# Plain neighbour sums of a graph network: one dense window over two batches of edge tiles instead of one

## The chip, the cores and the metric

The kernel runs on one core of a Trainium2 chip. The metric is the device time of one execution in microseconds (us). The engines named below are TensorE (PE in the rows; PEld is its weight load), VectorE (DVE), ScalarE (ACT), GpSimd (POOL) and SyncE (SP). A "q" behind an engine's name is its sequencer, the part that fetches instructions, computes registers, branches and waits.

## The reference, cut to what matters

Four graph layers run over one graph of 6,250 nodes and 106,250 edges, sorted by target node. The change is in the last layer, which has two plain sums over neighbours:

```python
def _sage_conv(x, src, dst, W_l, W_r, b):
    msg_sum = jax.ops.segment_sum(x[src], dst, num_segments=n)
    deg = jax.ops.segment_sum(jnp.ones_like(dst, dtype=x.dtype), dst, num_segments=n)
    mean = msg_sum / jnp.maximum(deg, 1.0)[:, None]
    return mean @ W_l.T + b + x @ W_r.T
h = jax.nn.relu(_sage_conv(x, src, dst, W1_l, W1_r, b1))
out = _sage_conv(h, src, dst, W2_l, W2_r, b2)
```

Both sums use the same edges; only `x` differs.

## The kernel before, in words

The edges are cut into 832 tiles of 128 edges, and 8 tiles (`G`) make a batch, so there are 104 batches. A table `meta` holds for each batch a flag, its first node, and the first node of each of its tiles. The sums `sums[feature, node]` stay in SBUF. Both rounds of the last layer are made by `mixed_round`, which every engine has in its own version; each handles batches in two ways.

**Sparse batches.** GpSimd gathers the 128 source rows of each tile from a table in HBM, with one indirect DMA a tile, eight a batch (`gather_mixed`, L747), into a ring of four buffers. ScalarE stages the indices three batches ahead (`stage`, L857). VectorE makes a one-hot matrix for each tile (`hot_sparse`, L2335), TensorE multiplies rows by one-hots and accumulates the eight tiles in one PSUM bank (`collect`, L1622), and VectorE adds the bank to `sums` (`add_sparse`, L2443).

**Dense batches.** Nothing is gathered. All node rows lie in SBUF as three bfloat16 parts (`XS`, 49 blocks of 128 nodes by 3 times 128 columns, made by `halve` and `halves` at the start of a round). For a tile, VectorE makes two one-hots: of the source's place in its block (`HOT_LO`, L2326, 128 columns) and of the pair (block, target's place in the tile) (`HOT_KEY`, L2327, `KEYS` = 50 x 16 = 800 columns). TensorE multiplies them in two matmuls of 400 columns (`build`, L1543): a count of edges for each source node and each of 16 targets. ScalarE copies these counts to `NEIGH[e]` as bfloat16 (`take_out`, L867), each tile into 16 columns of its own. When eight tiles are in place, TensorE multiplies `NEIGH` by `XS` in 49 matmuls of 384 columns (`apply`, L1550), in eight portions w = 0 to 7 of six (the last of seven). VectorE adds the three parts (`reduce`, L2367) and makes a matrix (`put`, L2372) with which TensorE moves each column to its node, adding up columns of the same node (`place_dense`, L1597); VectorE adds that to `sums` (`add_dense`, L2433).

**Order.** Batches 0, 3, 6 and so on are dense (34 of them), the other 70 are sparse. One step (`step`) handles one sparse batch and half a dense one: in PE's order it builds tiles of the *next* dense batch between portions of the present one, then collects the sparse batch. Two steps make a cycle of one dense batch `d`; a loop body holds four steps. VectorE follows in the same order: one-hots of the next dense tiles, the sum of the sparse batch before, one-hots of the next sparse batch in two halves (`hot_sparse`, parts 0 and 1), and the pieces of the root product (`ground`, L1606 to L1612 and L2459), of which there are 49, one a step. A sum to `sums` waits for `collect`; a `build` waits for its one-hots and for the copy two tiles before, since PSUM has two places for counts. Should a dense batch span more than 128 nodes, a slow path (`wide`) recounts it tile by tile.

**Registers.** A value of `meta` is brought into an engine's registers by `meta_of` (L558): one load for all values asked for, and then for each value a comparison with its bounds and an assertion. In `mixed_round` VectorE asks for one or two values at a time; ScalarE for none.

Of the kernel before, what the change touches and what calls it, by code (L numbers as in the profile page):

```python
# [19 lines left out]
FP32 = mybir.dt.float32  # L20
# [6 lines left out]
P = 128  # L27
# [26 lines left out]
KEYS = NHI * NEAR  # L54
DENSE = BATCHES // 3
SPARSE = BATCHES - DENSE
# [13 lines left out]
def build(nc, a, out):  # L70
    ctx = ExitStack()
    with ctx:  # L72
# [12 lines left out]
        tile_rows = nc.dram_tensor("tile_rows", [3, ROWB * P], INT32, kind="Internal").ap()  # L85
        one_over = nc.dram_tensor("one_over", [NODES_P, R16], FP32, kind="Internal").ap()
# [7 lines left out]
        ROOM = sb("ROOM", [P, 2 * NODES_P + 2048 + 2112 + 4096])  # L94
# [4 lines left out]
        TOUT = ROOM[:, 2 * NODES_P + 4160:].rearrange("p (b n) -> p b n", b=2)  # L99
# [48 lines left out]
        OHR = sb("OHR", [P, 2, G, R16], BF16)  # L148
# [48 lines left out]
        SPARE = sb("SPARE", [P, 8 * P + 48])  # L197
# [82 lines left out]
        def lin_rows(g):  # L280
# [16 lines left out]
        HOT_COLS = (P + KEYS) // 2  # L297
# [3 lines left out]
        NEIGH = [ROOM[:, low_room:low_room + NHI * P // 2].bitcast(BF16).rearrange("p (h s) -> p h s", s=P),  # L301
                 PACK[:, 0:NHI * P // 2].bitcast(BF16).rearrange("p (h s) -> p h s", s=P)]
        low_room += NHI * P // 2
        REST_X = [PACK[:, n * 4 * P:(n + 1) * 4 * P] for n in range(6)]
        RING_ROWS = [GB[:, 0, 0:G * P], GB[:, 1, 0:G * P], ROOM[:, low_room:low_room + G * P], ROOM[:, low_room + G * P:low_room + 2 * G * P]]
        hots = [SPARE[:, b * HOT_COLS:(b + 1) * HOT_COLS].bitcast(BF16) for b in range(2)]
        s_hot = PACK[:, NHI * P // 2:NHI * P // 2 + HOT_COLS].bitcast(BF16)
        HOT_LO, HOT_KEY = [h[:, 0:P] for h in hots], [h[:, P:P + KEYS] for h in hots]
        S_LO, S_KEY = s_hot[:, 0:P], s_hot[:, P:P + KEYS]
        lo_col, near_col = etype, key16  # L310
# [3 lines left out]
        bn = sb("bn", [P, CHUNKS, 6])  # L314
# [103 lines left out]
        class Mixed:  # L418


            def __init__(self, n, table, into, weights, bias, plus):
                self.n, self.table, self.into, self.weights, self.bias, self.plus = n, table, into, weights, bias, plus
                self.g0, self.d0, self.q0 = n * SPARSE, n * DENSE, n * XBLOCKS
                self.t0 = G * self.d0
                self.landed = [n * (16 * G) * len(range(c, SPARSE, RING)) for c in range(RING)]

        WIDE_D, WIDE_P = G * (10 + 2 * G + 2), G * (G + 2)
# [30 lines left out]
        mix_a = Mixed(0, t_l3a, H, "L3_gnn_W1_r", 0, None)  # L458
        mix_b = Mixed(1, t_l3b, X, "L3_gnn_W2_r", 1, X)
# [3 lines left out]
        mx_hot, mx_built, mx_out, mx_app = sem("mx_hot"), sem("mx_built"), sem("mx_out"), sem("mx_app")  # L463
# [105 lines left out]
        def batch_of(i, c):  # L569

            if isinstance(i, int) and i == DOUBLES:
                return 6 * i + c
            return 6 * i + (3 * (c // 2) + 1 + c % 2)
# [2053 lines left out]
```

## Time and profile before

| | us |
|---|---|
| median of 3 runs (6334.63 to 6341.05) | 6336.8 |
| the profiled execution | 6346.25 |
| its span, first to last instruction | 6344.3 |
| busy: PE, POOL | 4533.7 (71%), 4416.5 (70%) |
| busy: DVE, ACT | 2761.6 (44%), 1904.5 (30%) |
| granted TensorE clock, mean, as a share of full speed | 0.842 |

The span includes all four layers. The two rounds that the change is about lie between 4840 and 5565 us and between 5580 and 6305 us. A share of busy time says little by itself here: it averages over stages with different limits. Register, branch and semaphore instructions are not counted as busy at all, so an engine with little busy time may still be fully occupied by its sequencer.

### The profile page before, as it was taken

To read this page: it belongs to the slowest core of one execution; us is meant where nothing else is said; L and a number is where in the kernel's file an instruction comes from. 1 tells how busy PE (TensorE), PEld (TensorE's weight loads), DVE (VectorE), ACT (ScalarE), POOL (GpSimd) and SP (SyncE) were. 2 spreads that over 40 slices of the span, in tenths; PEclk is the share of its full clock that TensorE was granted. 3 is DMA by queue.
4 is the path that set the end of the run, shared out by engine and by line. 5 is a ranking of instruction groups with operands and counts; after the bars stand their busy time and mean duration, and the time that the engine had idled before them with its cause. 6 is when DMAs were issued, how large, how long until landed. Compare 5 with 4: busy or idle time off the path is not lost. (4 is left out here: it accounts for less than half of the span.)

```text
span 6344.3 us, 119904 instructions
## 1 busy us (share of the span) xinstructions
PE 4533.7 (71%) x27080; PEld 3709.3 (58%) x27081; DVE 2761.6 (44%) x10683; ACT 1904.5 (30%) x4793; POOL 4416.5 (70%) x4559
## 2 busy tenths in 40 slices
PE   3488887878778886566666675565555888778886
PEld 3377777767777775455555555555554555555554
DVE  6643333333333332566666542222225554355543
ACT  0022222222222223444444441111114333243332
POOL 3067777757777773777777647777775777767777
PEclk6599999999999997566666688878887999989998
DMA  3066666642222211333333322111121222222222
GB/s 79 3 168 161 156 154 156 158 119 53 53 53 53 53 52 44 89 83 83 83 83 83 71 63 52 52 52 52 52 52 52 54 53 54 53 63 54 54 53 59
DMA packets 380915, 478.11 MB, mean 75 GB/s; under 512 B 123697, under 2 KB 293202, under 8 KB 380242
## 3 DMA queue, kind: packets, MB, share of 16 engines
q0 software_dynamic: 142336, 295.20, 18.3%
q1 hardware_dynamic: 233778, 174.99, 10.9%
q14 instruction: 591, 4.84, 0.2%
q10 hardware_dynamic: 4128, 1.75, 0.1%
q8 instruction: 82, 1.34, 0.1%
HBM read 447.41 MB, written 24.15 MB: 74 GB/s over the span
## 5 line engine op out<-in xcount | busy, mean ns | idle before, releaser
L1320 PE MATMUL PS<-ROOM 128*128 128x128 f32 x8320 | 1028.4, 282 | 130.6 <-ACT ROOM L942 130.6
L1320 PEld LDWEIGHTS PS<-ROOM 128*128 128x128 f32 x8320 | 972.9, 195 | 200.5 <-ACT ROOM L942 147.7
L942 ACT COPY ROOM<-PS 128x512 f32<-128x512 f32 x1040 | 609.7, 586 | 1390.5 <-PE PS L1330 1387.1
L777 POOL DMA_INDIRECT GB<-table,IDX x832 | 793.0, 953 | 316.6 <-issue 252.1
L747 POOL DMA_INDIRECT GB<-table,IDX x576 | 571.4, 992 | 217.5 <-issue 174.4
L1969 DVE TENSOR_TENSOR ROOM<-ROOM,PS 128x128 f32 x312 | 89.7, 288 | 1362.7 <-PE PS L1338 1359.0
L777 POOL DMA_INDIRECT GB<-in_x,IDX x416 | 402.8, 968 | 370.7 <-ACT IDX L923 234.0
L747 POOL DMA_INDIRECT ROOM<-table,IDX x544 | 519.1, 954 | 165.8 <-issue 164.9
L1330 PE MATMUL PS<-OH,GB 128*128 128x256 f32 (+1 forms) x1664 | 387.9, 403 | 314.4 <-DMA GB<-table,IDX 253.0
L1330 PEld LDWEIGHTS PS<-OH,GB 128*128 128x128 f32 x1664 | 326.4, 248 | 361.3 <-issue 288.2
L735 POOL DMA_INDIRECT GB<-table_gat,IDX x416 | 426.6, 1025 | 127.7 <-issue 124.2
L735 POOL DMA_INDIRECT H<-table_gat,IDX x416 | 416.6, 1002 | 126.9 <-issue 121.4
L777 POOL DMA_INDIRECT H<-in_x,IDX x416 | 404.4, 972 | 126.8 <-issue 126.8
L777 POOL DMA_INDIRECT H<-table,IDX x416 | 397.3, 955 | 126.8 <-issue 124.1
L777 POOL DMA_INDIRECT ROOM<-table,IDX x416 | 396.4, 953 | 126.8 <-issue 124.1
L1463 PE MATMUL PS<-ROOM,OH 128*128 128x144 f32 x1664 | 431.9, 453 | 1.2 <-DVE ROOM L2120 1.2
L1463 PEld LDWEIGHTS PS<-ROOM,OH 128*128 128x128 f32 x1664 | 398.2, 332 | 2.8 <-issue 1.3
L1543 PE MATMUL PS<-SPARE 128*128 128x400 bf16 x1088 | 272.6, 344 | 164.0 <-DVE SPARE L2327 144.9
L1880 DVE SCALAR_TENSOR_TENSOR H<-iota_w,key,ROOM 128x256 f32<-128x256 f32 x416 | 173.9, 482 | 345.6 <-PE PS L1330 134.5
L1330 PE MATMUL PS<-OH,ROOM 128*128 128x128 f32 x832 | 171.7, 391 | 207.7 <-DMA ROOM<-table,IDX 207.7
L1550 PE MATMUL PS<-ROOM 128*128 128x384 bf16 x1666 | 311.5, 327 | 4.5 <-issue 2.5
L1550 PE MATMUL PS<-ROOM,PACK 128*128 128x384 bf16 x1666 | 310.2, 328 | 1.7 <-issue 0.3
(386 smaller groups left out, 8405.6 us busy)
## 6 DMA issues: line engine op xcount, KB each, us to landing
H<-one_over SPq DMA_DIRECT2D x416, 128.0 KB
ROOM<-one_over SPq DMA_DIRECT2D x416, 128.0 KB
ROOM<-local_row SPq DMA_DIRECT2D x104, 256.0 KB
GB<-table,IDX POOLq DMA_INDIRECT x1408
ROOM<-table,IDX POOLq DMA_INDIRECT x960
GB<-in_x,IDX POOLq DMA_INDIRECT x416
H<-in_x,IDX POOLq DMA_INDIRECT x416
H<-table,IDX POOLq DMA_INDIRECT x416
```

What stands on the lines that cost most here:

```text
L735: pool.indirect_dma_start(out=out[:, j, :], out_offset=None, in_=r.table.dram[:, :], in_offset=bass.IndirectOffsetOnAxis(ap=idx[:, j:j + 1 ...
L747: pool.indirect_dma_start(out=RING_ROWS[c][:, j * P:(j + 1) * P], out_offset=None, in_=m.table.dram[:, :], in_offset=bass.IndirectOffsetOn ...
L777: pool.indirect_dma_start(out=r.rows[c][:, j * P:(j + 1) * P], out_offset=None, in_=r.dram[:, :], in_offset=bass.IndirectOffsetOnAxis(ap=I ...
L942: act.copy(to.rearrange("p r (j d) -> p r j d", j=r.per), of.rearrange("p (j d r) -> p r j d", j=r.per, d=NEAR))\
L1320: ins = nc.tensor.matmul(PS[:, 4, 0:P], r.near[1 - b][:, t * P:(t + 1) * P], r.weights[:, t * P:(t + 1) * P], start=t == 0, stop=t == r.re ...
L1330: ins = nc.tensor.matmul(PS[:, n, j % r.per * r.cols:(j % r.per + 1) * r.cols], r.rows[c][:, j * P:(j + 1) * P], r.hot[b][:, j * r.cols:(j ...
L1463: ins = nc.tensor.matmul(PS[:, 1 - b, 0:MW_COLS], hot(1 - b)[:, j, :], MW[:, 1 - b, j, :], start=j == 0, stop=j == G - 1)
L1543: ins = nc.tensor.matmul(PS[:, 2 * b + a, 0:KEYS // 2], HOT_LO[b], HOT_KEY[b][:, a * KEYS // 2:(a + 1) * KEYS // 2], start=True, stop=True)
L1550: ins = nc.tensor.matmul(PS[:, 4 + e, 0:3 * P], NEIGH[e][:, h, :], XS[:, h, :], start=h == 0, stop=h == XBLOCKS - 1)
L1880: ins = dve.scalar_tensor_tensor(to, columns, key, WINDOWS[b][:, j * r.cols:(j + 1) * r.cols], ALU.is_equal, ALU.mult, accum_out=wstage[:, ...
L1969: dve.tensor_tensor(dst, dst, PS[:, 5, 0:P], ALU.add).then_inc(added, 1)
```

## The change

Of every four batches, the first two are now one dense **window** of 16 tiles (`PAIR`), and the other two are sparse: 26 windows and 52 sparse batches instead of 34 and 70. A cycle still has two steps and two sparse batches, but 16 dense tiles.

- A tile now counts for 12 targets (`SPAN`) instead of 16, so `KEYS` is 600, and `build` makes two matmuls of 300 columns.
- `NEIGH` has one column a node, so a tile's counts go to the column of its first node. `take_out` writes them at an offset that is only known at run time. The first column may be shared with the tile before: ScalarE leaves it out, and a new VectorE instruction adds it (`corrected`). `build` waits for that addition (`mx_cor`) instead of the copy.
- The offsets come from `meta`: in each step ScalarE and VectorE each load eight values (`offsets_of`), and VectorE two more in every second step.
- `HOT_LO` is made for four tiles in one `tensor_tensor`; `hot_sparse` is one `tensor_tensor` of 1024 columns instead of eight instructions of 128.
- The matrix of `put` becomes a plain shifted diagonal, cut at the window's last node; its bounds are worked out once, before the third layer's sums (new steps on `keyed`, a round trip of `span_row` through HBM by SyncE).
- GpSimd clears both `NEIGH` buffers once. The first round also builds the first window of the second round (`m.windows`), and the first window's `apply` follows the halving of `XS` portion by portion.

```diff
-KEYS = NHI * NEAR
-DENSE = BATCHES // 3
-SPARSE = BATCHES - DENSE
+SPAN = 12
+KEYS = NHI * SPAN
+PAIR = 2 * G
+CYCLE = 4
+DENSE = BATCHES // CYCLE
+SPARSE = BATCHES - 2 * DENSE
...
+        def offsets_of(engine, d, kk, low=0):
+
+            return meta_of(engine, window_of(d) * CYCLE + (2 + kk), 4 + G + low, G - low, P - 1)
...
         def tiles_of(w):
 
-            return (0, 1) if w == 0 else (w + 1,) if w < G - 1 else ()
+            return 2 * w, 2 * w + 1
...
-                def take_out(d, e, j):
+                def take_out(d, e, j, offsets):
...
-                    act.copy(NEIGH[e][:, :, j * NEAR:(j + 1) * NEAR].rearrange("p (a h) d -> p a h d", a=2),
-                             PS[:, 2 * b:2 * b + 2, 0:KEYS // 2].rearrange("p a (h d) -> p a h d", d=NEAR)).then_inc(mx_out, 1)
+                    if j == 0:
+                        act.copy(NEIGH_HALVES[e][:, :, :, 0:SPAN], counted_of(2 * b)).then_inc(mx_out, 1)
+                    else:
+                        act.copy(NEIGH_HALVES[e][:, :, :, bass.ds(offsets[j % G] + 1, SPAN - 1)],
+                                 counted_of(2 * b)[:, :, :, 1:SPAN]).then_inc(mx_out, 1)
...
+                    if more:
+                        offsets = offsets_of(act, d + 1, half)
...
-                    pe.wait_ge(mx_hot, d * G + (m.t0 + j + 1))
-                    if not isinstance(d, int) or m.t0 + d * G + j >= 2:
-                        pe.wait_ge(mx_out, d * G + (m.t0 + j - 1))
+                    pe.wait_ge(mx_hot, d * PAIR + (m.t0 + j + 1))
+                    if not isinstance(d, int) or m.t0 + d * PAIR + j >= 2:
+                        pe.wait_ge(mx_cor, d * PAIR + (m.t0 + j - 1))
...
                 def hot(d, j):
...
+                    b, q, n = j % 2, j // 4 % 2, window_of(d) * (CYCLE * G) + j
+                    if not isinstance(d, int) or m.t0 + d * PAIR + j >= 2:
+                        dve.wait_ge(mx_built, d * PAIR + (m.t0 + j - 1))
+                        dve.sem_inc(near_passed, 1)
+                    if j % 4 == 0:
+                        dve.tensor_tensor(HOT_LO[q], mid(iota_h[:, 0:P], 4), last(lo_col[:, bass.ds(n, 4)], P), ALU.is_equal)
                     dve.tensor_scalar(HOT_KEY[b], iota_h[:, :], near_col[:, bass.ds(n, 1)], None, ALU.is_equal).then_inc(mx_hot, 1)
 
+                def corrected(d, e, j, offset):
+
+                    dve.wait_ge(mx_out, d * PAIR + (m.t0 + j + 1))
+                    if j == 0:
+                        dve.sem_inc(mx_cor, 1)
+                        return
+                    dve.sem_inc(near_passed, 1)
+                    dve.wait_ge(mx_cor, d * PAIR + (m.t0 + j))
+                    column = NEIGH_HALVES[e][:, :, :, bass.ds(offset, 1)]
+                    dve.tensor_tensor(column, column, counted_of(2 * (j % 2))[:, :, :, 0:1], ALU.add).then_inc(mx_cor, 1)
...
-                    for j in range(part * G // 2, (part + 1) * G // 2):
-                        ins = dve.tensor_scalar(oh(b, j), iota_f[:, :], local[:, bass.ds(n + j, 1)], None, ALU.is_equal)
-                    if part == 1:
-                        ins.then_inc(mx_oh, 1)
+                    dve.tensor_tensor(OH[:, b, :].rearrange("p (j n) -> p j n", j=G), mid(iota_f[:, :], G),
+                                      last(local[:, bass.ds(n, G)], P), ALU.is_equal).then_inc(mx_oh, 1)
...
+                    if half == 0 and early:
+                        offsets = offsets_of(dve, d, 1, G - 2)
+                    for n, j in enumerate((G, G + 1) if half else (0, 1)):
+                        if more and not (m.n and first and half == 0):
+                            hot(d + 1, j)
+                        if early:
+                            corrected(d if half == 0 else d + 1, e if half == 0 else 1 - e, early[n], offsets[early[n] % G if half else n])
...
+                    if more:
+                        offsets = offsets_of(dve, d + 1, half)
+
+                    def next_tiles(low, high):
+                        for j in range(half * G + low, half * G + high):
+                            if more:
+                                hot(d + 1, j)
+                                corrected(d + 1, 1 - e, j - 2, offsets[(j - 2) % G])
+
+                    next_tiles(2, 4)
+                    if not isinstance(g, int) or g < XBLOCKS:
                         ground(g)
+                    next_tiles(4, 5)
+                    if not isinstance(g, int) or g + 1 < SPARSE:
+                        hot_sparse(i + (c + 1) // RING, (c + 1) % RING)
+                    next_tiles(5, 8)
```

## Rows read from the trace of the kernel before

**Rows 1.** Who GpSimd waited for, 4840 to 5600 us: total, times, longest.

```profile
POOL GB L747 <- issue: 89.3, 293, 0.3
POOL ROOM L747 <- ACT IDX L857: 0.3, 1, 0.3
```

**Rows 2.** TensorE timeline: start us, us, instruction; first round's first and last collect.

```profile
4874.89 1.14 PE L1550 MATMUL PS<-ROOM 128*128 128x384 bf16 x6
4875.87 1.95 PE L1622 MATMUL PS<-OH,GB 128*128 128x128 f32 x16
...
5559.59 3.78 PE L1622 MATMUL PS<-OH,GB 128*128 128x128 f32 x16 [5.04 <-DMA GB<-table,IDX]
```

**Rows 3.** Groups by line, 4840 to 5600 us: busy us, mean ns, idle before.

```profile
L2335 DVE TENSOR_SCALAR OH<-iota_w,local 128x128 f32<-128x128 f32 x560 | 126.0, 298 | 1.5 <-DVEq L2490 1.3 <-issue 0.2
L2327 DVE TENSOR_SCALAR SPARE<-iota_h,key 128x800 bf16<-128x800 f16 x274 | 119.6, 436 | 0.0
...
L867 ACT CAST ROOM<-PS 128x800 bf16<-128x800 f32 x136 | 110.5, 828 | 117.6 <-PE PS L1543 117.6
...
L2347 DVE TENSOR_TENSOR PACK<-X,ROOM 128x512 f32<-128x512 f32 x12 | 8.1, 682 | 0.0
```

**Rows 4.** Timeline of all engines from one collect to the next but one.

```profile
5010.08 1.95 PE L1622 MATMUL PS<-OH,ROOM 128*128 128x128 f32 x16
...
5016.78 0.51 PE L1543 MATMUL PS<-SPARE 128*128 128x400 bf16 x2 [1.02 <-DVE SPARE L2327]
...
5019.24 1.95 PE L1622 MATMUL PS<-OH,ROOM 128*128 128x128 f32 x16
...
5020.14 0.25 DVE L2326 TENSOR_SCALAR SPARE<-iota_h,etype 128x128 bf16<-128x128 f16 x1 [2.63 <-issue]
...
5020.81 0.42 DVE L2327 TENSOR_SCALAR SPARE<-iota_h,key 128x800 bf16<-128x800 f16 x1
...
5022.51 0.29 DVE L2443 TENSOR_TENSOR ROOM<-ROOM,PS 128x128 f32 x1 [0.62 <-issue]
...
5024.45 0.25 DVE L2326 TENSOR_SCALAR SPARE<-iota_h,etype 128x128 bf16<-128x128 f16 x1 [1.65 <-DVEq L2490]
...
5025.10 0.51 PE L1543 MATMUL PS<-SPARE 128*128 128x400 bf16 x2 [1.26 <-DVE SPARE L2327]
...
5025.44 1.14 PE L1550 MATMUL PS<-ROOM 128*128 128x384 bf16 x6
...
5027.15 0.51 PE L1543 MATMUL PS<-SPARE 128*128 128x400 bf16 x2
...
5030.01 1.95 PE L1622 MATMUL PS<-OH,GB 128*128 128x128 f32 x16
```

**Rows 5.** VectorE's groups by line over the whole span, two shapes near the new ones.

```profile
L1844 DVE TENSOR_TENSOR OH<-iota_w,local 128x1024 bf16<-128x1024 f32 x104 | 126.6, 1217 | 0.0
...
L2264 DVE TENSOR_TENSOR ROOM<-PS,ROOM 128x32 f32<-128x32 f32 x12 | 2.3, 191 | 0.4
```

**Rows 6.** Register loads, 400 to 1300 us: count, then ns min/median/max.

```profile
L558 SPq SEQ_ASSERT  x720: 18/18/18, 409.6 to 1298.4; - x180
...
L558 DVEq TENSOR_LOAD <-meta x180: 302/309/332, 406.8 to 1297.4; - x180
L558 SPq TENSOR_LOAD <-meta x90: 521/524/548, 408.8 to 1295.8; - x90
```

**Rows 7.** The same, 2600 to 3600 us.

```profile
L558 DVEq FUSED_REGOPS  x377: 81/190/196, 2608.2 to 3599.9; - x189
...
L558 DVEq SEQ_ASSERT  x282: 23/23/29, 2609.3 to 3591.1; - x141
...
L558 DVEq TENSOR_LOAD <-meta x95: 740/744/765, 2608.3 to 3599.1; - x95
```

**Rows 8.** Windows: length, busy us of PE, PEld, DVE, ACT, POOL; granted clock, DMA share, GB/s.

```profile
2550.00:2700.00 150.00, 97.25 (x508) 78.86 (x509) 92.26 (x417) 68.14 (x205) 115.23 (x115) 0.57 0.35 85
...
4950.00:5100.00 150.00, 131.80 (x860) 90.32 (x858) 75.39 (x299) 56.09 (x106) 113.72 (x120) 1.00 0.20 53
```

More of the change, by code:

```diff
@@ L550, in build @@
         N_PREP = SLOTS_AT + 2 + 15
+        KEYED = 23
+        lone = start[0:1, :]
+        gaps_of = lone[:, 0:DENSE * PAIR].rearrange("o (d k j) -> o d k j", d=DENSE, k=2)
+        most_of, least_of, wide_of, good_of, spans_of = (lone[:, (PAIR + n) * DENSE:(PAIR + n + 1) * DENSE] for n in range(5))
         PARTS_C = ((1, 1 + CHUNKS), (1 + CHUNKS, BATCHES // FOUR - 1))
@@ L755, in gather_mixed @@
                         one(RING * i + c, c)
-                for g in range(RING * DOUBLES, SPARSE):
-                    one(g, g % RING)
             def gather_gat(r):
@@ L805, in _ @@
             gather_near(near_c)
+            pool.wait_ge(added, 3 * BATCHES)
+            pool.wait_ge(span_in, 32)
+            for e in range(2):
+                pool.memset(NEIGH[e], 0.0).then_inc(emptied, 1)
             pool.wait_ge(norm_d, 1 + CHUNKS + 5)
@@ L2524, in mixed_round, with steps @@
-                for c in range(RING):
-                    step(DOUBLES - 1, c, False)
+                    return offsets if more else None
+                def steps(i):
+                    offsets = None
+                    for c in range(RING):
+                        offsets = step(i, c, offsets)
+                if m.n == 0:
+                    dve.wait_ge(span_in, 32)
+                    dve.tensor_scalar(dense_place[:, :], dense_place[:, :], pidx[:, 0:1], NO_NODE, ALU.is_lt, ALU.mult).then_inc(keyed, 1)
+                    dve.wait_ge(keyed, KEYED + 1)
+                    dve.tensor_scalar(dense_place[:, :], dense_place[:, :], pidx[:, 0:1], None, ALU.add).then_inc(keyed, 1)
+                    dve.wait_ge(keyed, KEYED + 2)
@@ new lines, in mixed_round @@
+                dve.wait_ge(xs_d, (m.n + 1) * 2 * GROUPS)
+                dve.wait_ge(xs_a, (m.n + 1) * 2 * GROUPS)
+                hot_sparse(0, 0)
+                steps(0)
+                with dve.Fori(1, DOUBLES - 1) as i:
+                    steps(i)
+                steps(DOUBLES - 1)
+                if m.windows > DENSE:
+                    offsets = offsets_of(dve, DENSE, 1, G - 2)
+                    for n in range(2):
+                        corrected(DENSE, 0, PAIR - 2 + n, offsets[n])
```

407 lines of the change are left out of this document (217 added, 190 removed).

## The prediction

> **What bounds the kernel now.** I read the page first (all engines' busy time and the slices), then the windows, and of the two changed rounds the waits of GpSimd, TensorE's collects, one cycle of the timeline, and last the register loads, which the page does not count as busy.
>
> GpSimd sets the pace of both rounds. Its only idle time between gathers is 0.30 us of issue; it waited once, for 0.3 us, for indices from ScalarE [rows 1]. A window of 150 us holds 119 gathers [rows 8], so 1.26 us each, 10.05 us a batch, 20.1 us a cycle of two sparse batches. From the first collect of the first round to its last are 5559.59 - 4875.87 = 683.7 us for 69 intervals of collects, 9.9 us each [rows 2]; the first ones are a little quicker because the engines behind GpSimd start late and catch up. The last collect waited 5.04 us for its rows to land [rows 2].
>
> But the engines behind GpSimd are close to it. In one undisturbed cycle the collects start at 5010.08, 5019.24 and 5030.01, and none of them waits for a transfer [rows 4]. TensorE's holes in it (1.02 and 1.26 us) are waits for one-hots from VectorE [rows 4]. And VectorE is not busy there, it is late: 2.63 us idle at the loop's end, with nothing waited for but issue; 0.62 us of issue before the sum, since two values are loaded into registers; 1.65 us after the sum, in which its sequencer leaves one branch, loads one flag and takes another branch [rows 4]. So the reader should see three paces: GpSimd 20.1 us a cycle, TensorE some 17 us of work, and VectorE's sequencer, which no busy column shows.
>
> **GpSimd's part.** 18 batches of 8 gathers fewer a round: 144 x 1.26 = 181 us less. If GpSimd still set the pace, the round's collects would span 25.5 cycles x 20.1 = 512 us instead of 684, both rounds together 343 us less. Whether it does is decided by what a cycle costs the others.
>
> **TensorE's part.** A portion of six products takes 0.98 us from its start to the next instruction [rows 2], 49 products 8.0 us; two collects 3.8; two roots 2 x 0.95 (5025.44 to 5027.15 is a portion and one of its parts, 1.71 us [rows 4]); placing 0.2. A build of 800 columns costs 0.34 us (5025.10 to 5025.44 [rows 4]); 600 columns about 0.25, and 16 of them 4.0 instead of 8 x 0.34 = 2.7. Sum 17.9 us a cycle, 16.6 before: still under 20.1.
>
> **ScalarE's part.** A copy of 800 columns took 828 ns [rows 3]; 550 to 600 should take 0.62, 16 of them 9.9 us, plus ground copies and its own register loads: some 18 us, beside the others. Not the longest, but each build now waits for copy and correction.
>
> **VectorE's part**, term by term for one cycle:
> - *Offsets.* Two loads of eight values. A load of one value takes 309 ns and one of three 744 [rows 6, 7]; yet SyncE loads eight in 524 ns (720 assertions to 90 loads) [rows 6]. So eight values take 0.5 us if VectorE behaves as SyncE, 1.8 if its time grows as from one to three. Then each value costs a 190 ns register operation and a 23 ns assertion [rows 7], 1.7 us for eight, and the steps from one to the next. From 2.2 to 3.5 us; I take 3.0. Two: 6.0 us. These lie in the sequencer, whose instructions follow one another: behind them stand the one-hots of tiles 2 to 7 (or 10 to 15), for which TensorE waits.
> - *Other loads.* Two values more for tiles 14 and 15, and flag and base of two sparse batches: 3 x 1.2; the base of the dense sum 0.6; flag and branch 1.65 [rows 4]: 5.9 us, of which 1.3 are new.
> - *Tiles.* For each the key one-hot (436 ns at 800 columns [rows 3], 0.37 at 600) and the correction of 50 elements (nearest shape with PSUM 191 ns [rows 5]; the strided shape is not in the trace, at most twice that). The sequencer needs several operations for each, with the two explicit waits that the edit adds. Between successive tiles 0.7 us, an estimate from the 0.17 us or so that each such operation took between instructions 5020.14 and 5020.81 (four instructions [rows 4]) and the added ones: 16 x 0.7 = 11.2 us. Bounds 0.57 (the engine's own 0.37 + 0.2) and 0.9.
> - *`HOT_LO`* four times like a `tensor_tensor` of 512 (682 ns [rows 3]): 2.4 us. *`hot_sparse`* two of 1217 ns [rows 5] instead of 16 of some 0.21 (298 ns each, overlapped [rows 3]): 2.4 instead of 3.4, but now in one piece ahead of tile 5's one-hot.
> - *Reduce, put, three sums, two ground copies, loop end* (2.63 / 2): 3.9 us.
>
> Sum 6.0 + 5.9 + 11.2 + 4.8 + 3.9 = 31.8 us, against some 14 before. Engine and sequencer overlap by perhaps 4, so the floor is 28 us before any wait. That is above GpSimd's 20.1 and above 684 / 25.5 = 26.8, the cycle from which the round is slower than now.
>
> The Trainium skill ("Advanced Engine Details and Errata", Sequencer Loop) says that other engine instructions can be read and queued while control work executes, which would hide the loads. The trace does not bear that out where it matters: 1.65 us of idle VectorE around one loaded flag [rows 4]. By that rule the cycle would lose both offset loads.
>
> **The waits between them.** I walk a cycle from the start of tile 7's one-hot, t = 0. *Second half:* build 7, portion 3, place, dense sum at 2.1; collect to 3.75. One-hots 8 and 9 and corrections 6 and 7 to 4.3; two-value load, then the sum 1.7 later (as 5020.81 to 5022.51 [rows 4]), 5.7; offsets to 9.0; one-hot 10 ready at 9.7. TensorE has been idle since 5.5. Tile 11 at 10.7, portion and root to 12.7, ground copy 12.95, `HOT_LO` and key of tile 12 to 14.3, `hot_sparse` to 15.7, tile 13 to 16.1, portion to 17.35, tiles 14, 15 and the last portion to 19.05, collect to 20.95: 17.2 us for this half. *First half:* load of two offsets, tiles 0 and 1 and the last corrections to 20.9, reduce, put, sum 22.8, branch 24.5, offsets 27.5, one-hot 2 at 28.2 (TensorE idle since 22.7), tile 3 and its portion 30.6, root and copy 31.55, tile 4 at 32.95, `hot_sparse` and tile 5 to 34.9, two portions, place and collect to 39.7: 18.75 us. Loop end 1.3 on average. Together 37.3 us; I take 37.5, since TensorE is then busy half of the time, and the clock was 0.57 where it was busy 97 of 150 us against 1.00 at 132 [rows 8]. Only portions and roots on this path feel it.
>
> **Outside the cycles.** The first round's first window has 16 tiles instead of 8, with corrections and two offset loads: +13 us before its first collect; the second round has it ready and saves some 6. The `keyed` steps add about 15 small instructions of one partition, taken at 0.3 us each, 5 us if nothing hides them. Clearing `NEIGH` lies beside VectorE's statistics of the third layer; uncovered it would be some 6 us. I add 17 us in all, with room for the last portion of waits. The slow path is not taken: the drawn edges give windows of 116 to 125 nodes and 6 to 10 nodes a tile, inside its limits of 128 and 11.
>
> **The sum.** A round: 25.5 x 37.5 = 956, less 684, +272.5; two rounds +545; +17: +562 us. The profiled execution would go from 6346.3 to 6908, and as it stands 9.5 us above the median, the median from 6336.8 to 6899, rounded 6900.
>
> **Rivals.**
> 1. *VectorE's loads and register work overlap with its queued instructions*: 37.5 - 6 - 1.5 = 30 us a cycle, 25.5 x 30 = 765, 2 x 81 + 17 = +179: 6516. For it: before the sum only 0.62 of the 1.2 us of a two-value load shows. Against: the offsets come right after a wait for TensorE, when nothing is queued.
> 2. *More stalls like the 2.63 us at the loop's end*, inside a loop body that grows by a good part: two more a body, 2.6 us a cycle, +133: about 7030. The Trainium skill ("Advanced Engine Details and Errata", ISA Cache) gives sequencers a small store of instructions in two lines, which would make a longer body miss more often; the trace shows such a stall once a body.
> 3. *Faster: the pair is hidden.* If offsets are cheap and a tile costs VectorE only 0.5 us, TensorE (17.9 us and its holes, about 3 before) or GpSimd sets 20.1 to 22 us: 25.5 x 22 = 561, 2 x -123 + 17 = -229: 6108; at GpSimd's pace 6011. It decides below 26.5 us a cycle (26.8 less the 17 us). For it: GpSimd loses 26% of its gathers, and VectorE is busy only 75 of 150 us [rows 8]. Against: the floor of 28.
> 4. *The slow path is taken after all* (a table entry that I read wrongly): far above 7200.
>
> **How the numbers follow.** Chances: forecast 0.58, rival 1 0.15, rival 2 0.13, rival 3 0.10 with what lies near no change, rival 4 0.04. Per-cycle bounds: 29.7 us (tile 0.57, offsets 2.2, more overlap) gives 25.5 x 29.7 = 757, 2 x 73.7 + 17 = +164, 6500; 43 us (tile 0.9, offsets 3.5, stalls, slower clock) gives 2 x 413 + 17 = +843, 7180. The range 6500 to 7180 takes in rival 2 and half of rival 1 and leaves out about 2 in 10. Faster by over 0.2% (13 us, what a measurement can tell) 0.09, within 0.02, slower 0.89.
>
> **What would show it.** Right: collects 17 to 20 us apart; GpSimd waiting for ScalarE's indices, some 17 us a cycle; TensorE's largest wait for VectorE's key one-hot behind a gap of VectorE of 3 us or more after each sparse sum, with the register line ahead of it; eight-value loads on VectorE of 0.5 to 1.8 us; granted clock under 1.00 in these rounds. Wrong: collects 10 to 11 us apart, GpSimd still waiting for issue alone. A correction of over 0.4 us, or a copy at a run-time offset much over 0.62, would shift the path to ScalarE without changing the sign.

## The result and the profile after

| | before | after |
|---|---|---|
| median of the runs made together (4 each) | 6338.33 us | 7095.59 us |
| span of the profiled execution | 6344.3 us | 7087.4 us |
| busy PE, DVE, ACT, POOL | 71%, 44%, 30%, 70% | 66%, 42%, 28%, 59% |
| granted TensorE clock, mean | 0.842 | 0.799 |

The changed kernel takes 1.119 times as long (95% interval 1.118 to 1.121), 757 us more. Forecast were 6900 us, +562, with a range of 6500 to 7180. The sign, the mechanism and the range were right; the size fell 196 us short. (The profiled execution of the kernel before lay 8 us above its median and that of the changed kernel 6 us below, so the two spans differ by 743 us and the medians by 757.)

**Where the time went.** TensorE's timeline, first and last collect of the first round and last collect of the second (start us, length, instruction):

```profile
4887.82 3.30 PE L1673 MATMUL PS<-OH,GB 128*128 128x128 f32 x16
...
5944.36 1.95 PE L1673 MATMUL PS<-OH,ROOM 128*128 128x128 f32 x16
...
7045.28 1.95 PE L1673 MATMUL PS<-OH,ROOM 128*128 128x128 f32 x16
```

The first round spans 1056.5 us where it spanned 683.7 [rows 2]; the second starts its collects at 6000.91 and spans 1044.4, before 685.2. That is +732.0 of the +743.1 us between the two spans. Outside the rounds lie only 11.1 us: the first collect is 11.9 us later, and the stretches between the rounds and behind them are equal within a microsecond.

Within a round the collects of the loop are 23.85, 20.65, 20.5 and 20.3 us apart, and this repeats: 85.3 us for two cycles, 42.65 for one. GpSimd, which waited once for 0.3 us before [rows 1], now stands idle most of the time. Its waits from 4840 to 5960 us (total, times, longest):

```profile
POOL ROOM L786 <- ACT IDX L898: 286.3, 25, 15.9
POOL GB L786 <- ACT IDX L898: 251.8, 24, 11.7
```

**One half.** The timeline of the changed kernel from one collect to the next, some of its lines:

```profile
5308.17 1.95 PE L1673 MATMUL PS<-OH,GB 128*128 128x128 f32 x16
...
5311.07 1.14 PE L1602 MATMUL PS<-ROOM 128*128 128x384 bf16 x6
5312.47 0.29 DVE L2539 TENSOR_TENSOR ROOM<-ROOM,PS 128x128 f32 x1 [1.80 <-issue]
...
5315.98 0.38 DVE L2409 TENSOR_SCALAR SPARE<-iota_h,key 128x600 bf16<-128x600 f16 x1 [3.22 <-issue]
...
5316.56 0.38 DVE L2409 TENSOR_SCALAR SPARE<-iota_h,key 128x600 bf16<-128x600 f16 x1
...
5316.78 0.42 PE L1595 MATMUL PS<-SPARE 128*128 128x300 bf16 x2 [4.58 <-DVE PACK L2420]
...
5317.36 0.66 PE L1595 MATMUL PS<-SPARE 128*128 128x300 bf16 x2 [0.16 <-DVE PACK L2420]
...
5317.81 2.12 PE L1602 MATMUL PS<-ROOM 128*128 128x384 bf16 x6
...
5320.30 0.68 PE L1663 MATMUL PS<-bias_rows,ones_mat 1*128 1x128 f32 x2
5321.12 0.29 DVE L2555 COPY H<-PS 128x128 f32 x1 [3.91 <-PE PS L1663]
...
5324.94 2.12 PE L1602 MATMUL PS<-ROOM 128*128 128x384 bf16 x6
...
5328.85 1.95 PE L1673 MATMUL PS<-OH,GB 128*128 128x128 f32 x16
```

What the reader is to see: the two engines take turns. After the sum (5312.47) VectorE's sequencer loads the offsets, and the engine stands for 3.22 us with nothing waited for but issue. Since 5312.2 TensorE has had nothing to do: it waits 4.58 us for the one-hot and the correction (the wait names only the last of them). Then it is VectorE that waits, 3.91 us, for the root product that stands behind TensorE's build and portion. And the portion behind each gap takes 2.12 us for the same six products that took 1.14 at 5311.07. From 4950 to 5850 us this holds for the second and the third portion of all 42 halves; the first and the last are mostly at 1.14. The granted clock was 1.00 ahead of the gap (first line; columns as in [rows 8]) and 0.50, the lower of its two levels (1.2 GHz, against 2.4), over the portion and the root product behind it (second line). The other two lines are long windows; before, the clock was 1.00 in this round:

```profile
5308.00:5312.00 4.00, 3.91 (x31) 2.98 (x29) 2.06 (x6) 0.84 (x3) 0.60 (x1) 1.00 0.14 35
5317.30:5320.30 3.00, 2.94 (x11) 1.68 (x11) 0.00 (x0) 1.45 (x3) 0.34 (x1) 0.50 0.00 0
...
4950.00:5100.00 150.00, 94.19 (x450) 55.26 (x448) 58.27 (x153) 41.52 (x79) 57.35 (x56) 0.74 0.10 26
5250.00:5400.00 150.00, 93.61 (x445) 55.06 (x445) 57.78 (x153) 41.09 (x78) 54.73 (x56) 0.77 0.10 25
```

VectorE's groups by line, 4900 to 5850 us (busy us, mean ns, idle before), and its register instructions from 4950 to 5900 us (ns min/median/max):

```profile
L2409 DVE TENSOR_SCALAR SPARE<-iota_h,key 128x600 bf16<-128x600 f16 x360 | 142.6, 396 | 202.7 <-issue 179.7 <-PE PS L1595 21.3
...
L2420 DVE TENSOR_TENSOR PACK<-PACK,PS 128x50 f32 x171 | 63.5, 372 | 13.1 <-ACT PACK L913 11.7
...
L2428 DVE TENSOR_TENSOR OH<-iota_w,local 128x1024 f32<-128x1024 f32 x45 | 57.0, 1266 | 0.0
```

```profile
L579 DVEq FUSED_REGOPS  x688: 53/183/190, 4950.2 to 5896.9; - x172
L579 DVEq SEQ_ASSERT  x537: 23/23/33, 4951.2 to 5897.2; - x179
L579 DVEq TENSOR_LOAD <-meta x156: 305/539/606, 4950.4 to 5896.6; - x156
```

The longest load is that of eight values, 606 ns, close to SyncE's 524 [rows 6]; with its register operations and assertions one such load ends 2.82 us after it begins, on ScalarE 2.40. TensorE's waits from 4900 to 5850 us (total, times, longest) show that its hole before a build is VectorE's.

```profile
PE PS L1595 <- DVE SPARE L2409: 144.8, 69, 4.4
PE PS L1595 <- DVE ROOM L2420: 105.0, 63, 4.1
PE PS L1595 <- DVE PACK L2420: 94.8, 44, 4.6
```

The end of the round shows what the root product is worth in its place. There are 49 pieces of it and 52 steps, so the last three steps have none, while all eight builds of a step are still there:

```profile
5899.09 1.95 PE L1673 MATMUL PS<-OH,GB 128*128 128x128 f32 x16
...
5914.22 1.95 PE L1673 MATMUL PS<-OH,GB 128*128 128x128 f32 x16
...
5929.32 1.95 PE L1673 MATMUL PS<-OH,ROOM 128*128 128x128 f32 x16
```

These halves take 15.1 us instead of 20.5, though a root product keeps TensorE busy for only some 1.6 us and VectorE for 0.3.

### The profile page after: what moved, and what is told of

Read it like the earlier page. It is cut to its first block and busy times, and to the rows that moved or that the text cites. A ratio compares the mean times of both kernels' runs of the same rounds, so it can differ in the third digit from the quotient of the medians.

```text
span 7087.4 us, 125605 instructions
## 1 busy us (share of the span) xinstructions
PE 4704.9 (66%) x26264; PEld 3720.0 (52%) x26265; DVE 2956.1 (42%) x10331; ACT 2014.3 (28%) x5046; POOL 4170.4 (59%) x4273
## 3 DMA queue, kind: packets, MB, share of 16 engines
q10 hardware_dynamic: 4128, 1.75, 0.1%
## 5 line engine op out<-in xcount | busy, mean ns | idle before, releaser
L814 POOL DMA_INDIRECT GB<-table,IDX x832 | 791.7, 952 | 317.1 <-issue 251.1
L1595 PE MATMUL PS<-SPARE 128*128 128x300 bf16 x1664 | 426.4, 366 | 815.8 <-DVE SPARE L2409 374.5
L786 POOL DMA_INDIRECT GB<-table,IDX x416 | 429.2, 1032 | 679.2 <-ACT IDX L898 488.4
L786 POOL DMA_INDIRECT ROOM<-table,IDX x416 | 413.7, 995 | 684.2 <-ACT IDX L898 560.0
L1595 PEld LDWEIGHTS PS<-SPARE 128*128 128x128 bf16 x1664 | 144.1, 111 | 1048.5 <-DVE SPARE L2409 904.5
L2409 DVE TENSOR_SCALAR SPARE<-iota_h,key 128x600 bf16<-128x600 f16 x832 | 326.7, 393 | 467.4 <-issue 399.8
L814 POOL DMA_INDIRECT ROOM<-table,IDX x416 | 395.8, 952 | 126.8 <-issue 125.0
L913 ACT CAST PACK<-PS 128x550 f32 x390 | 257.2, 659 | 636.7 <-PE PS L1595 525.1
L913 ACT CAST ROOM<-PS 128x550 f32 x390 | 256.7, 658 | 579.8 <-PE PS L1595 475.5
```

What stands on the lines that cost most here:

```text
L786: pool.indirect_dma_start(out=RING_ROWS[c][:, j * P:(j + 1) * P], out_offset=None, in_=m.table.dram[:, :], in_offset=bass.IndirectOffsetOn ...
L814: pool.indirect_dma_start(out=r.rows[c][:, j * P:(j + 1) * P], out_offset=None, in_=r.dram[:, :], in_offset=bass.IndirectOffsetOnAxis(ap=I ...
L913: act.copy(NEIGH_HALVES[e][:, :, :, bass.ds(offsets[j % G] + 1, SPAN - 1)], counted_of(2 * b)[:, :, :, 1:SPAN]).then_inc(mx_out, 1)
L1595: ins = nc.tensor.matmul(PS[:, 2 * b + a, 0:KEYS // 2], HOT_LO[j // 4 % 2][:, j % 4, :], HOT_KEY[b][:, a * KEYS // 2:(a + 1) * KEYS // 2], ...
L2409: dve.tensor_scalar(HOT_KEY[b], iota_h[:, :], near_col[:, bass.ds(n, 1)], None, ALU.is_equal).then_inc(mx_hot, 1)
```

## The experiments

Each is an edit of the changed kernel, and its median stands against 7095.6 us; ratios are to the kernel before, run beside it (6337.5 to 6349.6 us). A half is the distance between two collects, a cycle is two halves, and their times are those of the loop's first round in the profiled execution. The kernel before ran 11 to 12 us longer beside four of the runs (no correction, ScalarE alone constant, more fillers, combined) than beside the others, so a difference of medians between groups is good to about 12 us; where it matters the ratios are the better measure.

### The offsets

**Constant offsets**: ScalarE and VectorE load no offsets and use constants, so counts go to other columns than the table says.

```diff
-            return meta_of(engine, window_of(d) * CYCLE + (2 + kk), 4 + G + low, G - low, P - 1)
+            return [7 * (kk * G + low + n) for n in range(G - low)]
```

> The changed kernel with the column offsets as constants (7 columns a tile) on ScalarE and VectorE: no load of eight or two offsets, no assertions on them, no run-time addresses; counts go to wrong columns, all other work is the same. Changed kernel: 7096 us, 42.7 us a cycle. Theory (the offset loads on VectorE stand on the path, and the gaps that they open halve TensorE's clock behind them): 3 us less a half for the load and 2 to 3 more for the clock, about 31.5 us a cycle, 6530 us. Rival (the chain one-hot, build, copy, correction sets the pace and the loads lie beside it): at most 1 us a half less, above 6990 us.

Measured: 6659.1 us (ratio 1.051), 436 us less; a cycle of 34.1 us, 8.5 less, at a granted clock of 0.84. Theory had 6530 and the rival above 6990: the gain is three quarters of the theory's, and the rival is out.

**No assertions**: the same loads of offsets, without the register operation and the assertion for each value.

```diff
-            return meta_of(engine, window_of(d) * CYCLE + (2 + kk), 4 + G + low, G - low, P - 1)
+            return meta_of(engine, window_of(d) * CYCLE + (2 + kk), 4 + G + low, G - low, P - 1, "cut to the bound when the table was made")
```

> The changed kernel, complete, only without the bounds assertions on the loaded offsets (8 x 0.28 us a load); the loads stay. Theory: 2.2 us a half less, and the clock recovers in part: 36 to 38.5 us a cycle, 6750 to 6880 us. If the load from memory itself is the cost: no change, 7090. If neither is on the path: no change.

Measured: 6749.8 us (1.065), 346 us less, a cycle of 35.9 us. In its trace the 0.60 us load of eight values (at 5300.83) is followed within 0.04 us by the operations of the next tile. So most of what the offsets cost (346 of 436 us) is not the load but the register operations and assertions that follow for each value.

**ScalarE alone constant**: VectorE still loads; ScalarE's copies go to other columns.

```diff
+            if engine is nc.scalar:
+                return [8 * (kk * G + low + n) for n in range(G - low)]
             return meta_of(engine, window_of(d) * CYCLE + (2 + kk), 4 + G + low, G - low, P - 1)
```

> ScalarE alone takes constants for its eight offsets, VectorE still loads them: columns are copied to other places than the table says. Theory (ScalarE's loads, 2.4 us each, run beside VectorE's 2.8 us and end no later): 7080 to 7110 us, no change. Rival (ScalarE is the later of the two, and the builds wait for its copies): up to 2.4 us a half, 4.8 a cycle, 6850 us.

Measured: 7100.8 us (1.119): nothing. ScalarE's load of the same values, almost as long, is hidden; VectorE's is not. The loss is in one engine's sequencer, not in the table or in reading it twice.

### The correction

**No correction**: the addition of the shared column is left out. VectorE still waits for ScalarE's copy before it raises the semaphore, so this tries the addition alone and not the chain of build and copy.

```diff
-                    dve.wait_ge(mx_cor, d * PAIR + (m.t0 + j))
-                    column = NEIGH_HALVES[e][:, :, :, bass.ds(offset, 1)]
-                    dve.tensor_tensor(column, column, counted_of(2 * (j % 2))[:, :, :, 0:1], ALU.add).then_inc(mx_cor, 1)
+                    dve.sem_inc(mx_cor, 1)
```

> VectorE's addition of the shared column (16 a cycle) is left out, and what waited for it waits for the key alone; sums of nodes shared by two tiles come out without their second part. Theory (the correction starts 0.15 us behind its key and takes 0.37, so a tile's pitch is 0.15 to 0.37 us less without it, and offsets and clock stay): 16 x 0.15 to 16 x 0.37 = 2.4 to 5.9 us a cycle, 6850 to 7000 us. Rival (the correction is what makes the cycle long, since each build waits for it): 8 us a cycle and more, under 6800 us.

Measured: 6974.9 us (1.098), 121 us less or 2.4 us a cycle: 16 times 0.15 us, the lower end of the theory. The rival is out. But the granted clock fell with it, from 0.76 to 0.71 between 4950 and 5500 us, so part of what the addition costs may be hidden in this number; that was not taken apart. And the expectation misread one distance: the correction starts 0.28 to 0.29 us behind the start of its key (5315.98 and 5316.27 in the changed kernel); 0.15 us is from there to the next key, where VectorE is not held up.

### TensorE's clock

The next three add useless small matmuls in a gap of TensorE, ahead of the builds that wait for VectorE. They write a PSUM column that nobody reads.

```diff
+                        if w % 4 == 1:
+                            for _ in range(FILLERS):
+                                nc.tensor.matmul(PS[:, 4 + e, 3 * P:4 * P], XS[:, 0, 0:P], XS[:, 0, 0:P], start=False, stop=False)
                         if more and not (first and half == 0):
```

**Fillers** (`FILLERS = 40`).

> The changed kernel with 40 small matmuls (128 columns, into an unread part of the bank that TensorE sums into) ahead of the second pair of builds in each half, where TensorE otherwise waits 4 to 5 us; more work, nothing taken away. Theory (half clock behind the gap costs 2 to 3 us a half): the portion behind the gap runs at the full clock, about 37.5 us a cycle, 6830 us. Rival (the clock behind the gap costs nothing, since VectorE sets the pace): 7095 us or slower.

Measured: 7025.9 us (1.109). A miss, 70 us less where the theory had 265: the 40 took only 2.40 us and left a gap of 0.7 to 2.5 us. From 4950 to 5850 us the portion behind this gap was at full clock (1.14 us) in 26 of 44 halves, as at 5406.01 behind a gap of 1.23 us, and at about 2 us in 12. What stayed slow was the third portion, behind the second gap: 39 of 44. The next expectation took two halves between 5312 and 5352 us, in which both portions were slow, for the rule.

**More fillers** (`FILLERS = 76`).

> 76 small products instead of 40 stand ahead of the builds that wait for VectorE's offsets; nothing else is changed against the changed kernel. The 40 left 1.6 to 1.9 us of TensorE's gap open, and the portions behind it stayed at half clock. Theory (TensorE's clock falls in the 4 to 5 us gap, and the work behind it pays): the 76 take some 4.5 us, the gap is closed, portions of six products take 1.1 us again and not 2, a cycle 37.5 to 38 us instead of 42.7, 6830 us in all. Rival (the gap has nothing to do with the clock, the work behind it is slow for another reason): portions stay at 2 us, a cycle 41 to 43 us, 6990 to 7100 us.

Measured: 7000.6 us (1.103), inside the rival's range, but not for the rival's reason. The 76 close the gap and the portion behind them is at full clock:

```profile
5312.41 4.41 PE L1702 MATMUL PS<-ROOM 128*128 128x128 bf16 x76
...
5317.84 1.14 PE L1603 MATMUL PS<-ROOM,PACK 128*128 128x384 bf16 x6
...
5321.47 0.42 PE L1596 MATMUL PS<-SPARE 128*128 128x300 bf16 x2 [1.86 <-DVE ROOM L2424]
...
5323.08 0.42 PE L1596 MATMUL PS<-SPARE 128*128 128x300 bf16 x2 [1.19 <-DVE SPARE L2413]
...
5323.34 2.01 PE L1603 MATMUL PS<-ROOM,PACK 128*128 128x384 bf16 x6
```

The next portion, behind two more gaps (1.86 and 1.19 us), is again slow. From 4950 to 5850 us the second portion is at full clock in all 47 halves and the third at about 2 us in 32 of 45. So the clock is lost twice a half, and I had filled one place.

**Both gaps**: 24 and 16 matmuls more ahead of the two builds behind the root product.

```diff
+                        for nth, j in enumerate(tiles_of(w) if more and not (first and half == 0) else []):
+                            if w % 4 in (1, 2):
+                                for _ in range((76, 0, 24, 16)[2 * (w % 4 - 1) + nth]):
+                                    nc.tensor.matmul(PS[:, 4 + e, 3 * P:4 * P], XS[:, 0, 0:P], XS[:, 0, 0:P], start=False, stop=False)
+                            build(d + 1, j)
```

> The 76 small products of more fillers, and 24 and 16 more of them in the second gap of a half, between the root product and the builds of the two tiles behind it. More fillers held the clock for the first portion and the root (1.14 and 0.38 us instead of 2.12 and 0.63) but not for the portion behind the second gap (2.0 us), and took a half from 20.7 to 19.3 us. Theory (each gap costs its own stretch at half clock, some 1.4 us): a half of 18 us, 2.6 us a cycle less than more fillers, 7000 - 25 x 2 x 2.6 = 6870 us. Rival (what was left there is VectorE's sequence and the clock is off its path): 6980 to 7020 us, no change against more fillers.

Measured: 6918.6 us (1.092), 177 us less than the changed kernel. The clock is held:

```profile
4950.00:5100.00 150.00, 129.40 (x1383) 101.88 (x1380) 65.11 (x175) 44.91 (x86) 67.65 (x64) 0.98 0.12 31
5250.00:5400.00 150.00, 130.08 (x1401) 102.96 (x1402) 64.32 (x173) 44.68 (x85) 63.37 (x60) 0.97 0.11 29
```

The second, third and fourth portions are at full clock in all of some 47 halves. Three of four halves are 17.8 to 18.3 us; the one with the loop's end is 23.5. There TensorE waits up to 4.2 us of issue, and the first portion behind it is often at half clock (10 of 48). The gain over more fillers is 82 us by the medians and 71 by the ratios, less than the 130 of the theory. Of the 85 us between the two spans 15 lie ahead of the first collect, 12 in the first round, where the half with the loop's end is some 1.5 us longer than with more fillers, and 55 in the second, where it is not. Idle matmuls are a probe here, not a remedy.

### Who waits for whom

**Portions first**: all four portions of a half and the root product ahead of the builds of its last six tiles.

```diff
+                    if building:
+                        for j in tiles_of(4 * half):
+                            build(d + 1, j)
...
                     for w in range(4 * half, 4 * half + 4):
-                        if more and not (first and half == 0):
-                            for j in tiles_of(w):
-                                build(d + 1, j)
                         apply(d, e, w)
-                        if w % 4 == 1 and with_ground:
-                            ground(t)
+                    if with_ground:
+                        ground(t)
+                    if building:
+                        for w in range(4 * half + 1, 4 * half + 4):
+                            for j in tiles_of(w):
+                                build(d + 1, j)
```

> The changed kernel, complete, with TensorE's order changed: in each half two builds, then all four portions of products and the root, and only then the other six builds. Theory: TensorE does useful work during VectorE's register loads, so portions leave the path and the gap shrinks; VectorE and ScalarE then pace the six builds alone, about 32 us a cycle, 6550 us. If VectorE's sequencer alone set the pace and the portions were not on the path: no change, 7095.

Measured: 6682.2 us (1.054), 413 us less, a cycle of 34.1 us (theory 6550 us and 32). TensorE's work now fills the time of VectorE's loads.

**Root early**: the root product stands behind the first portion of a half instead of the second; one condition changed.

```diff
-                        if w % 4 == 1 and with_ground:
+                        if w % 4 == 0 and with_ground:
                             ground(t)
```

> The changed kernel with one line moved: the root product stands behind the first portion of a half instead of the second, so ahead of the builds that wait for VectorE's offsets. VectorE waited 3.9 us a half for it before the copy of the ground block, while four one-hots stood behind that copy. Theory (the two engines wait for each other in turn, and this wait is a part of the sum): VectorE goes on at once, TensorE's portion is still behind, so 2 to 3.5 us a half, 4 to 7 a cycle, 6740 to 6890 us. Rival (TensorE's order of portions sets the half anyway, and VectorE then waits for the build or the copy instead): 7050 to 7110 us.

Measured: 6693.0 us (1.056), 403 us less from one condition, more than the theory's 200 to 350. Its timeline, one half:

```profile
5312.18 1.95 PE L1673 MATMUL PS<-OH,GB 128*128 128x128 f32 x16
...
5320.14 0.81 DVE L2409 TENSOR_SCALAR SPARE<-iota_h,key 128x600 bf16<-128x600 f16 x2 [4.75 <-issue]
5321.06 0.29 DVE L2555 COPY H<-PS 128x128 f32 x1
5321.84 2.12 PE L1602 MATMUL PS<-ROOM,PACK 128*128 128x384 bf16 x6
...
5325.10 1.59 PE L1602 MATMUL PS<-ROOM,PACK 128*128 128x384 bf16 x6
...
5328.56 1.95 PE L1673 MATMUL PS<-OH,ROOM 128*128 128x128 f32 x16
```

The half is 16.4 us instead of 20.7. The copy at 5321.06 waits for nothing. VectorE's next one-hots are then ready while TensorE works at its portion, the second gap is gone, and the portion behind it is partly back at full clock: 1.59 us here, 1.14 in the half before, instead of 2.12 (at full clock in 31 of 50 halves, where it was in none). The first gap is little changed, 3.5 to 3.9 us instead of 3.9 to 4.6. So the half lost 4.3 us, somewhat more than the 3.9 us wait itself; by the portion, 0.5 us or more of it is clock.

### Together

**Combined**: portions first, and no assertions on the loads of offsets, flags and bases in these rounds.

> The portions ahead of the builds of the same half (as in portions first), and no bounds assertions on the loads of offsets, flags and bases of the mixed rounds. Portions first took a cycle to 34.4 us, leaving the assertions on the offsets out took 1.5 to 2.7 us off each load. Theory (the two add, since VectorE's sequencer sets the pace in either): 34.4 - 2 x 1.7 - 6 x 0.2 for the smaller loads = 29.8 us a cycle, 6680 - 25 x 4.6 x 2 = 6450 us. Rival (with the clock held TensorE is the bound in portions first, and shorter loads don't show): 6600 to 6680 us.

Measured: 6619.6 us (1.043): the rival's side. The loads show less (VectorE's idle time of issue ahead of a key falls from 212.6 us in portions first to 71.1, 4900 to 5850 us), and VectorE now waits 95.1 us, 2.0 a half, for a root product that stands behind all four portions.

**Root ahead**: combined, the root product ahead of the portions, and VectorE's offsets loaded ahead of the sparse sum.

```diff
+                    ahead = offsets_of(dve, d + 1, half) if more else None
                     if not (first and half == 0):
...
-                    if more:
-                        offsets = offsets_of(dve, d + 1, half)
+                    offsets = ahead
```

> Portions first and no assertions as in the combined kernel, and two edits more: VectorE loads a half's offsets before it waits for the sparse sum, and TensorE computes the root product ahead of the four portions instead of behind them. In the combined kernel a half took 15.2 us, and VectorE waited 1.9 to 2.5 us of it for the root product, and 1.3 to 2.3 us lay between the sum and its next one-hot. Theory (VectorE's sequence and its waits for TensorE set the pace, and GpSimd and TensorE have room): 15.2 - 1.9 - 0.8 = 12.5 to 13 us a half, 25.5 to 27.5 us a cycle with the loop's end, 6250 to 6370 us. Rival (TensorE's portions, 4.4 us, and the chain of build, copy and correction set it whatever the order): 14 to 15 us a half, 6520 to 6620 us.

Measured: 6647.8 us (1.049, interval 1.047 to 1.050): nearer the rival, whose range ended at 6620, and 28 us slower than combined. The wait for the root is gone, and in its place VectorE waits for the builds behind the block of portions, up to 5.1 us (4900 to 5850 us):

```profile
DVE SPARE L2414 <- PE PS L1596: 152.3, 56, 5.1
```

A block of 24 matmuls takes 4.1 us (5305.30 to 5309.37), and for that time no tile moves on.

**Three edits**: root early, no assertions, offsets loaded ahead, with the portions left between the builds.

> The root product behind the first portion as in root early (portions stay between the builds), no bounds assertions on the mixed rounds' loads, and VectorE's offsets loaded before it waits for the sparse sum. Root early measured halves of 15.7 to 16.4 us and 20 with the loop's end, 34.1 us a cycle; the one-hot behind the offsets was still 4.8 us late. Theory (what is left is the stretch of offsets in VectorE's sequence): the assertions go (1.5 us and more a half, as in no assertions), part of the load hides behind the sum's wait, clock holds better: 13.5 to 14.5 us a half, 29 to 30 us a cycle, 6400 to 6460 us. Rival (as in the other order, the chain of one-hot, build, copy and correction is the pace once the offsets are early): 15 us a half, 6560 to 6640 us. In neither is it faster than the kernel before, which needs 26.8 us a cycle.

Measured: 6330.7 us (11 runs; before 6337.7 in 15), ratio 0.9989 with an interval of 0.9980 to 0.9998. A miss of both theory and rival, on the good side: a cycle is 26.85 us where I expected 29 to 30. TensorE's timeline for a half, and a window:

```profile
5207.78 1.95 PE L1674 MATMUL PS<-OH,GB 128*128 128x128 f32 x16
...
5210.80 1.14 PE L1603 MATMUL PS<-ROOM 128*128 128x384 bf16 x6
...
5214.16 1.14 PE L1603 MATMUL PS<-ROOM 128*128 128x384 bf16 x6
...
5217.38 1.14 PE L1603 MATMUL PS<-ROOM 128*128 128x384 bf16 x6
...
5219.40 1.30 PE L1603 MATMUL PS<-ROOM 128*128 128x384 bf16 x7
...
5220.54 1.95 PE L1674 MATMUL PS<-OH,GB 128*128 128x128 f32 x16
```

```profile
5250.00:5400.00 150.00, 115.25 (x717) 73.54 (x718) 90.73 (x250) 65.34 (x124) 86.21 (x90) 0.97 0.15 40
```

12.8 us this half, with every portion at full clock; TensorE's largest hole ahead of a build is 1.31 us in it. From 4950 to 5500 us, 8 of 164 portions are still at about 2 us. The miss has a plain cause: the single edits had brought 403 us (root early) and 346 us (no assertions), together 749, and the three together brought 765. I had put 1.5 us a half on the assertions where their own run had shown 3.4 (42.65 to 35.9 us a cycle). With that the forecast would have been 34.1 - 6.8 = 27.3 us a cycle, and 26.85 was measured. The granted clock went from 0.84 and 0.85 in the single edits to 0.97, but no more than 16 us beyond the sum are left for it, the loads ahead and the other assertions together.

## Why the prediction was right, and which term was mis-sized

- **GpSimd off the path, the pair on it**: right. GpSimd waits for ScalarE's indices, which in the program wait for the collects, 538.1 / 49 = 11 us a half, 22 a cycle against "some 17", since the cycle is longer. (The row of [rows 8] counts 120 gathers and not 119, so 1.25 us each; no sum changes by it.)
- **Offsets, 3.0 us each, not overlapped**: right (2.82 us; 3.22 us of idle VectorE). Rival 1 falls. By the sentence of the Trainium skill ("Advanced Engine Details and Errata", Sequencer Loop) other engine instructions can be read and queued while control work executes, which would have hidden these loads. Constant offsets show that they cost 8.5 us a cycle with all that follows from them: VectorE had ended the sum of 5312.47, its last instruction ahead of the load, before the load began at 5312.82. In three edits, where the loads stand ahead of the wait for the sum, how much of them is hidden was not taken apart.
- **Tile, 0.7 us**: too much. Undisturbed, successive keys start 0.44 to 0.58 us apart (5315.98 and 5316.56 above). The correction takes 372 ns, within the bound of twice 191, but overlaps with the keys around it: leaving it out is worth 0.15 us a tile, at the lower clock named above.
- **`hot_sparse` and `HOT_LO`**: 1266 and 692 ns, as taken (1217, 682).
- **The walk**: with the clock held, in both gaps, three halves of four measure 17.8 to 18.3 us; the walk gave 17.2 and 18.75, a mean of 18.0. That mean is closer than either half, which is luck, but the order of events is as walked: in both gaps, from a collect at 5307.29 on, the ready key, the ground copy, `hot_sparse` and the third portion come within 0.5 us of the walk's times.
- **The clock, "37.3 us; I take 37.5"**: this is the term that was mis-sized. The prediction saw that TensorE would be busy only half of the time, had the row with clock 0.57 beside it, said that portions and roots on this path feel it, and then put 0.2 us a cycle on it. A half has two portions behind a gap (2.12 - 1.14 = +0.98 us each), a root (0.63 and 0.68 us for its two parts against 0.38 and 0.48) and two or three builds (0.66 against 0.42), and VectorE waits for most of them. 5.15 us a cycle were missing. Two halves without the loop's end take 41.0 us in the changed kernel and 36.2 with the clock held in both gaps, where the walk had 35.95: 4.8 us is the clock, and some 0.4 the loop's end (1.7 us a cycle against 1.3). The cycle as a whole fell by only 3.8 us in both gaps, to 38.85, since the half with the loop's end gained almost nothing there. Times 25.5 and two rounds the missing 5.15 us would be 263, of which the cheaper intervals at both ends took 74 back (the last three of a round, for one, have no root product, and in the second round the last two have no tiles to build): the rounds span 2100.9 us against a forecast of 2 x 956 = 1912, 189 more.
- **The Trainium skill** ("TensorE: Matmul & The Clock Gate", HAM oscillation) describes a matmul kernel in which every wait of TensorE for a DMA throws its clock back to the lower level, so that each stage starts slow, and advises to restructure the loop so that the engine's clock stays up. The waits here are for VectorE and not for a DMA, but the trace agrees on what follows them: 2.12 us against 1.14 for the same six products, twice in every half.
- **Outside, +17**: measured +11.1. The first collect is 11.9 us later (forecast 13); the second round saves nothing.
- **Rival 2, more stalls of issue**: not needed. One stall a loop body remains, 23.85 against 20.5 us, so 3.3 us where the forecast had 2.6. **Rival 3, the pair hidden**: not in this order of instructions. But its threshold, 26.8 us a cycle, was near: three edits has 26.85 and takes as long as the kernel before. That it fits so well is in part luck, since 25.5 such cycles would be 685 us and the rounds span 671.8 and 664.2; the 33 us gained in them against the kernel before are partly lost again outside, where the first collect is 13.9 us later.

What stays open: whether the kernel before gains from leaving out its own assertions in these rounds was not measured, so 6330.7 us is no proof that the window itself is worth its place; even as it stands, 7 us in 6338 are a tie for practical purposes. Constant offsets and no assertions differ by 1.8 us a cycle; how that splits between the load and the clock was not taken apart. The second gap was never filled alone, the offsets were never loaded ahead alone, and the stall at the loop's end was not tried.

## What to carry to other kernels

Before moving work onto an engine with idle time, count what its sequencer does for it: a value brought into a register with a checked bound cost (2.82 - 0.61) / 8 = 0.28 us beside the load, eight of them 2.8 us with it, and none of it is in the busy column. Then look for who waits in the gap, and put into it work that is ready (here a root product, one condition changed, 403 us of 757). When a gap opens in front of TensorE, look in a row like it for the clock behind it and price the work there by that row; with the first of two gaps filled, the portion behind the second was still slow in most halves. And when you combine edits, start from what each of them measured alone, not from the term that it was planned with.

## What the hardware showed that was not expected

- The same load of eight values costs VectorE 2.82 us and ScalarE 2.40 us, some 600 and 550 ns for the load and the rest for the values; on ScalarE leaving it out changed nothing (7100.8 against 7095.6 us).
- Not only the gaps of 4 to 5 us: two of 1.86 and 1.19 us, one behind the other, were followed by a portion of 2.01 us. With 40 fillers, a gap of the same 1.75 to 1.77 us behind them was followed by a portion at full clock five times and at half clock twice, so the length of that gap alone did not decide it. In three edits the granted clock of two windows of 150 us was 0.99 and 0.97, with TensorE busy 112 to 115 us of them; in the changed kernel it was 0.74 and 0.77 with 94.
- 76 matmuls of 128 columns a half, with the sole purpose of keeping the clock, took 4.41 us and made the kernel 95 us faster; 116 in both gaps, 177 us.
